# Residual of the one-class tiles: from a VectorE addition to an accumulating scatter into a destination filled beforehand

## What is computed

```
x = x + 0.5 * ffn(layernorm(x), W1, b1, W2, b2)
x = x + attn(layernorm(x), W_toP, W_U, W_F, W_V, W_lam, B_mat, C_mat, W_fromP)
x = x + 0.5 * ffn(layernorm(x), W1, b1, W2, b2)

def ffn(x, W1, b1, W2, b2):              # 8 experts, 128 -> 512 -> 128
    h   = mod(int(x[:, :2].sum(axis=1)), 8)
    sel = [h, mod(h + 1, 8)]             # the class h of a token names its two experts
    return sum over e of  (e in sel) / 2 * (relu(x @ W1[e] + b1[e]) @ W2[e] + b2[e])
```

## Time and profile before

| | us |
|---|---|
| median of three runs | 600.19 |
| lowest and highest run | 599.95, 601.44 |
| span of the profiled execution | 598.6 |
| of it: setup until the first matmul of the first feed-forward stage | 63.0 |
| first feed-forward stage until the last scatter landed | to 269.4 |
| attention stage and second sort | to about 386 |
| second feed-forward stage | to the end |

### The profile page before, as it was taken

The page is one execution under the profiler, slowest core; times in us unless marked ns, Lnnn a source line. Parts: engine busy times, 40 slices in busy tenths (PEclk is TensorE's granted clock), DMA queues, the critical chain, the costliest instruction groups (busy, mean ns, idle before and its releaser), DMA issues.

```text
span 598.6 us, 15962 instructions
## 1 busy us (share of the span) xinstructions
PE 514.1 (86%) x5269; PEld 437.2 (73%) x5269; DVE 432.9 (72%) x1026; ACT 296.2 (49%) x494; POOL 321.1 (54%) x410
## 2 busy tenths in 40 slices
PE   0278899999999999956799836999999999999990
PEld 0136599999999999942466614689999999999980
DVE  6899677777777777746876779677777777777760
ACT  2384655555555556412988400155555655555540
POOL 3014847777777767350016610447777677777543
PEclk9996999999999999997999967699999999999996
DMA  9980111112111112109003380111121111112100
GB/s 244 328 340 11 41 34 50 47 47 50 48 51 43 51 41 53 31 30 266 16 1 72 72 142 1 28 38 46 51 50 48 44 46 47 48 51 51 36 24 18
DMA packets 37850, 40.96 MB, mean 68 GB/s; under 512 B 5813, under 2 KB 30731, under 8 KB 37266
## 3 DMA queue, kind: packets, MB, share of 16 engines
q1 hardware_dynamic: 27698, 21.65, 13.5%
q0 software_dynamic: 9088, 17.87, 11.5%
q10 hardware_dynamic: 992, 0.44, 0.3%
HBM read 23.00 MB, written 17.83 MB: 68 GB/s over the span
## 4 chain that ended last, share of the span: by engine, by line
PE 69%; DVE 14%; issue 5%; DMA 3%; ACT 3%; POOL 3%; SPq 2%; POOLq 0%; DVEq 0%
PE ps L774 19%; PE ps L756 10%; PE ps L758 10%; PE ps L757 10%; PE ps L776 10%; PE ps L792 2%; SPq L366 2%; PE ps L680 2%; PE ps L728 2%; DMA X<-in_L_attn_x 1%; DVE X L1122 1%; DVE bn L1101 1%; POOL G L478 1%; DVE onehot_b L987 1%; PE ps L836 1%
## 5 line engine op out<-in xcount | busy, mean ns | idle before, releaser
L1047 DVE SCALAR_TENSOR_TENSOR hlo<-ps,hhi 128x1024 f16<-128x1024 f32 x144 | 174.1, 1209 | 103.0 <-ACT hhi L586 103.0
L586 ACT ACTIVATE hhi<-ps 128x1024 f16<-128x1024 f32 x144 | 145.7, 1012 | 170.1 <-PE ps L758 170.1
L774 PE MATMUL ps<-w2s,hhi 128*128 x1136 | 202.3, 273 | 0.0
L776 PE MATMUL ps<-w2s,hlo 128*128 x1136 | 194.9, 219 | 0.0
L478 POOL DMA_INDIRECT G<-rows,places x142 | 141.9, 1000 | 88.2 <-issue 40.2
L756 PE MATMUL ps<-xhi,w1s 128*128 128x256 f16 (+1 forms) x736 | 168.0, 248 | 3.9 <-DVE xlo L1041 2.1
L758 PE MATMUL ps<-xhi,w1s 128*128 128x256 f16 (+1 forms) x736 | 168.0, 248 | 0.0
L757 PE MATMUL ps<-xlo,w1s 128*128 128x256 f16 (+1 forms) x736 | 167.9, 248 | 0.0
L774 PEld LDWEIGHTS ps<-w2s,hhi 128*128 128x128 f16 x1136 | 111.1, 98 | 12.1
L776 PEld LDWEIGHTS ps<-w2s,hlo 128*128 128x128 f16 x1136 | 111.1, 98 | 1.3
L486 POOL DMA_INDIRECT x1d<-O,places x71 | 71.3, 1004 | 41.6 <-issue 29.1
(11 more groups left out here) (240 smaller groups left out, 509.5 us busy)
## 6 DMA issues: line engine op xcount, KB each, us to landing
rows<-X SPq DMA_DIRECT2D x2, 2080.0 KB, 12.0
rows<-X SPq DMA_DIRECT2D x4, 1040.0 KB, 7.6
X<-in_L_attn_x SPq DMA_DIRECT2D x8, 512.0 KB, 8.0
X<-x1d SPq DMA_DIRECT2D x8, 512.0 KB, 7.4
G<-rows,places POOLq DMA_INDIRECT x142, 2.6
w1r<-in_L_ffn_W SPq DMA_DIRECT2D x1, 2048.0 KB, 11.3
x1d<-O,places POOLq DMA_INDIRECT x71, 2.3
out<-O,places POOLq DMA_INDIRECT x71, 2.3
```

What stands on the lines that cost most here:

```text
L586: nc.scalar.activation(hhi[tile.k][e][:, :, 0:tile.cols], H[e][:, :, 0:tile.cols], ACT.Relu).then_inc(hi_done[e], 1)
L774: nc.tensor.matmul(Y[tile.k][:, s, :], hhi[tile.k][e][:, c, tok], w, start=first, stop=False, skip_group_check=True)
L776: ins = nc.tensor.matmul(Y[tile.k][:, s, 0:P], hlo[tile.k][e][:, c, tok], wh, start=False, stop=(e == 1 and c == CH - 1), skip_group_check ...
L1047: v.scalar_tensor_tensor(out=hlo[tile.k][e][:, :, c], in0=H[e][:, :, c], scalar=0.0, in1=hhi[tile.k][e][:, :, c], op0=ALU.max, op1=ALU.sub ...
```

## The change

The destination of each scatter is filled with the stage's input before the stage. In the first stage SP copies x from DRAM to `x1d` in one DMA of 4 MB behind the bias parts; in the second SP stores each quarter of X to `out` behind the quarter of `rows`. POOL waits for these copies (`seeded`) after its first eight gathers. For a pure tile the scatter then has an add as its compute operation, so that it adds O to the row in DRAM, and it has no bounds check; DVE's `residual` is left out, and the first step of `collect` takes b2 of the class, spread over both sub-tiles, in place of O. The class's table entry and the wait for the old scatter move with it to `collect`. G of a pure tile is free once `xn` is made. Mixed tiles go on as before.

```diff
+            sp.dma_start(x1d, x.rearrange("b t d -> (b t) d")).then_inc(seeded[0], 16)
             sp.wait_ge(rows_out[0], 32)
+            sp.wait_ge(seeded[0], SEEDED[0])
...
                 sp.dma_start(rows_t[:, s, :], X[:, s, :]).then_inc(rows_out[1], 16)
+                sp.dma_start(out_t[:, s, :], X[:, s, 0:D]).then_inc(seeded[1], 16)
...
                     for s in range(tile.subs):
+                        if tile.pure:
+                            nc.gpsimd.indirect_dma_start(
+                                out=dst, out_offset=bass.IndirectOffsetOnAxis(
+                                    ap=places[:, tile.at, SUB + s:SUB + s + 1], axis=0),
+                                in_=O[tile.slot][:, s, :], in_offset=None,
+                                compute_op=ALU.add).then_inc(scat[tile.slot], 16)
+                            continue
...
                 pool.wait_ge(back_ready, 1 + r)
+                pool.wait_ge(seeded[r], SEEDED[r])
...
-                            pool.wait_ge(res_done, (tile + (AHEAD - SLOTS)).done())
+                            old = tile + (AHEAD - SLOTS)
+                            if old.pure:
+                                pool.wait_ge(xn_ready, old.done())
+                            else:
+                                pool.wait_ge(res_done, old.mixed_done())
...
+                def residual(tile):
+                    if tile.pure:
+                        return
+                    at = ready(tile)
+                    dve.wait_ge(gath[tile.slot], tile.moved())
                     for s in range(tile.subs):
                         ins = v.tensor_tensor(O[tile.slot][:, s, :], G[tile.slot][:, s, 0:D],
-                                              b2v[:, bass.ds(at[0 if tile.pure else s], D)], ALU.add)
+                                              b2v[:, bass.ds(at[s], D)], ALU.add)
                     ins.then_inc(res_done, 1)
...
                     o, y = O[tile.slot][:, 0:tile.subs, :], Y[tile.k][:, 0:tile.subs, :]
+                    base = o
+                    if tile.pure:
+                        base = b2v[:, bass.ds(ready(tile)[0], D)][:, None, :].to_broadcast([P, SUB, D])
                     dve.wait_ge(y_ready, tile.done())
-                    v.scalar_tensor_tensor(out=o, in0=y[:, :, 0:P], scalar=scl[:, 2:3], in1=o, op0=ALU.mult,
+                    v.scalar_tensor_tensor(out=o, in0=y[:, :, 0:P], scalar=scl[:, 2:3], in1=base, op0=ALU.mult,
                                            op1=ALU.add).then_inc(y_half, 1)
```

More of the change, by code:

```diff
@@ L68, in macaron_kernel @@
         rows_t = rows[1:N + 1, :].rearrange("(t p) d -> p t d", p=P)
+        out_t = out.rearrange("b t d -> (b t) d").rearrange("(t p) d -> p t d", p=P)
+        SEEDED = (16, 16 * (NPAIR // 2))
         x1_t = x1d.rearrange("(t p) d -> p t d", p=P)
@@ L237, in macaron_kernel @@
         table_ready = sem("table_ready")
+        seeded = [sem("seeded0"), sem("seeded1")]
         gath = [sem(f"gath{k}") for k in range(SLOTS)]
@@ L293, in done, with mixed_done @@
                 return self.r * NJ + self.j + 1
+            def mixed_done(self):
+                return self.r * MIXED + sum(not Tile(self.r, j).pure for j in range(self.j + 1))
             def moved(self):
@@ L391, in _ @@
                 sp.dma_start(rows_t[:, s, :], X[:, s, :]).then_inc(rows_out[1], 16)
+                sp.dma_start(out_t[:, s, :], X[:, s, 0:D]).then_inc(seeded[1], 16)
             sp.wait_ge(rows_out[1], 16 * NPAIR // 2)
+            sp.wait_ge(seeded[1], SEEDED[1])
             for k in range(SLOTS):
@@ L1049, in low, with ready @@
                                            op1=ALU.subtract).then_inc(lo_done[e], 1)
-                def residual(tile):
-                    at = load(tile.at)
+                def ready(tile):
                     if r == 0 and tile.j == 0:
                         dve.wait_ge(b2_ready, 1)
-                    dve.wait_ge(gath[tile.slot], tile.moved())
                     if tile.j >= SLOTS:
                         dve.wait_ge(scat[tile.slot], (tile + -SLOTS).moved())
+                    return load(tile.at)
+                def residual(tile):
[3 more added lines that the diff above has]
+                    dve.wait_ge(gath[tile.slot], tile.moved())
                     for s in range(tile.subs):
                         ins = v.tensor_tensor(O[tile.slot][:, s, :], G[tile.slot][:, s, 0:D],
-                                              b2v[:, bass.ds(at[0 if tile.pure else s], D)], ALU.add)
+                                              b2v[:, bass.ds(at[s], D)], ALU.add)
                     ins.then_inc(res_done, 1)
```

## The result

| | before | after |
|---|---|---|
| median, us | 600.17 | 620.78 |
| lowest and highest run | 599.95, 601.44 | 619.76, 621.8 |
| ratio, 95% interval | | 1.0342, [1.0324, 1.0359] |
| span of the profiled execution | 598.6 | 619.8 |

The changed kernel is 3.4% slower, some 20 us, far above the forecast of 602.7 and above the range's end of 611.0. The direction was foreseen, the size was not. Of the four runs of the changed kernel two lie near 619.9 and two, the profiled one among them, near 621.7, with a mean granted clock of 0.948 to 0.949 and of 0.943. What follows reads the trace after in the order of the groups of before.

The account below looks back on a forecast made before the run. PE was taken to bound the feed-forward bodies, with POOL close behind. Terms of 0 for the bodies, 0.8 for the tails and 1.7 for the head gave +2.5 us on 600.19, so 602.7, range 599.8 to 611.0.

Parts of the forecast that it names:

- d: Extra POOL issue time of one accumulating scatter over a plain one: taken as +0.1 us, bounded by -0.03 and +1.0.
- POOL as the bound above a threshold: Rival, feed-forward bodies: above d = 0.21 each stage grows by 50 d - 10.4, 621 at d = 0.4; chance 0.15.
- The spare time: POOL in the body: 0.29 us to spare for a tile, 10.4 us over 36 tiles, covering 50 d = 5.
- the lead of the gathers: Body: gathers are issued more than two tiles before ACT needs them, so landings of twice 2.1 us are covered.
- The tail: End of each stage: four of POOL's last seven scatters accumulate, 4 d = 0.4 us for a stage, 0.8 for both.
- The head, +1.7: Start of the first stage: the copy to x1d ends at 61.8, delays tile 0's gathers, costs PE 1.7 us.
- the prediction's other assumption: Copy to x1d: reading and writing cost as much as the slower alone, 9.7 to 14.3 us, ending at 52 to 57.
- The residual: DVE in the bodies: pure tiles lose two additions each, 28.2 us in all, hidden beside PE's work, worth 0.
- The moved waits: G's release by ACT's normalising and the later wait for the old scatter: zero cost.
- the copies to `out`: Before the second feed-forward stage: four stores of 1 MB, covered by 27 us before its first gather, zero cost.
- The last signs that the prediction named: Accumulating scatter's mean against 1007 ns, POOL's idle time ahead of a scatter (0.29 us to spare), ACT waiting for gathers.

## Why the prediction was wrong

**The step that failed is the size of d.** It was bounded by -0.03 and +1.0, and 0.1 was taken, near the low end, because gather and scatter differ by 0.03. That likeness says how little direction and check cost; both rows are plain copies, and neither says anything of an add. The runs showed 0.59, six times the term. With it the prediction's own rival, POOL as the bound above a threshold, became the case, and it had a chance of 0.15. Between bounds that far apart, with a threshold between them and no row of the operation, nearness to a cheap relative was too weak a reason.

**The spare time was a second error, the other way.** The 0.29 us of a tile are right: from the first scatter to the last gather POOL's idle time beyond 0.30 sums to 8.97 us, near the 10.4 taken. What was left out is the lead of the gathers. POOL in the kernel before has three long waits and two shorter ones behind its last gather (237.16), 10.74 us beyond 0.30 in all:

```profile
237.16 0.99 POOL L478 DMA_INDIRECT G<-rows,places  x1 [0.30 <-issue]
...
244.96 0.98 POOL L486 DMA_INDIRECT x1d<-O,places  x1 [3.25 <-PE ps L758]
...
255.80 0.98 POOL L486 DMA_INDIRECT x1d<-O,places  x1 [3.10 <-PE ps L758]
```

This time can be used too, because POOL may fall behind before anyone waits. In the changed kernel its last gather is 16.0 us late, and ACT's last `xn` only 8.8; before and after:

```profile
247.97 0.49 ACT L600 ACTIVATE xn<-G 128x127 f32<-128x127 f32 x1
```

```profile
253.11 1.02 POOL L488 DMA_INDIRECT G<-rows,places  x1 [0.30 <-issue]
```

```profile
256.74 0.49 ACT L622 ACTIVATE xn<-G 128x127 f32<-128x127 f32 x1 [1.68 <-DMA G<-rows,places]
```

The prediction knew this lead ("more than two tiles before ACT needs it") and used it for the transfers alone, not for POOL. So the threshold is at d = 0.39 and not at 0.21. By the rival's formula, 50 d - 10.4, the measured d would have given 19 us for a stage and about 640 in all; its 621 for d = 0.4 is near the result by luck, because the two errors offset each other.

**The tail** was priced as 4 d, 2.3 us at the measured d, and lost 4.1. The rest is a queue: DVE's end finds POOL with five scatters to issue, where it was three with a fourth just begun.

**The head, +1.7, was wrong.** The copy was done before the first gather's data. Stretches of the setup after, columns as in rows 8:

```profile
42.00:44.00 2.00, 0.00 (x0) 0.00 (x0) 1.97 (x4) 2.00 (x2) 0.00 (x0) 1.00 1.77 587
...
54.00:56.00 2.00, 2.00 (x4) 0.96 (x4) 1.75 (x5) 2.00 (x2) 2.00 (x2) 0.50 0.04 8
```

```profile
60.48 0.88 ACT L622 ACTIVATE xn<-G 128x127 f32<-128x127 f32 x2 [1.19 <-DMA G<-rows,places]
```

A stretch counts a packet where it starts, which is how the DMA share comes to 1.77. The trace has the copy as 64 packets of 64 KB: the first starts at 42.3, the last starts at 53.1 and ends at 55.6. So 4.19 MB took 13.3 us, 315 GB/s. Reading and writing did not each cost their own time, and the prediction's other assumption (9.7 to 14.3 us, an end at 52 to 57) was right. SP issued the copy at 37.44, and the profile has its landing 20.0 us later, at 57.4, still ahead of the first gather's data: ACT starts at 60.48, as in rows 10. The transposes of tile 2 start at 70.12 where it was 69.77, but at 69.72 in the kernel without the add, which has the same copy. The Trainium skill, page "DMA: Bandwidth & Descriptors", section "Latency and other measured facts", has 207 GB/s for copies between DRAM tensors in tiles of 128 x 16 KiB at a row pitch of 512 KiB, and 214 at its best pitch. This copy, in runs of 64 KB, went 1.5 times as fast; no run here has the page's layouts.

**What held.** The residual is worth nothing in time, shown by the kernel without the add; DVE's busy time fell by 22 us, not 28: the additions' group fell by 24.1 (34.3 us for 142 of them, 10.2 for 42), since two in a row overlap, and the other 1.8 us are not accounted for. The moved waits and the copies to `out` cost nothing. The last signs that the prediction named were the right ones to look at: the scatter's mean, the idle time ahead of it, and ACT's wait for gathers.

## What to carry to other kernels

An indirect DMA with an add isn't a scatter with a free addition: here it costs POOL 1.6 times the issue of a plain one, and the engine that writes descriptors may be the one that stands closest behind the bound. Before work is moved to such an engine, sum its idle time from the first instruction that will grow to the end of the stage, less the gap that every issue has, and divide by the number of those instructions: that is the price from which it decides. Idle time behind the engine's last gather counted here because the gathers have a lead, about 9 us. If the new instruction's price isn't in the trace and its bounds lie on both sides, measure it or move only as many as the upper bound allows. Here 12 of 25 tiles were free and 25 cost 20 us.

## What the runs showed of the hardware

- The accumulating indirect scatter of 128 rows of 512 B takes 1.59 to 1.60 us on POOL, the plain one 1.01, without bounds check 0.99. With 64 rows the accumulating one takes 1.44. The queue's packets show what is written. These are the rows of POOL's queue (packets, MB, share of 16 engines' span) of the kernel before, the changed one, and the one with 64 rows:

```profile
q0 software_dynamic: 9088, 17.87, 11.5%
```

```profile
q0 software_dynamic: 20288, 17.87, 20.1%
```

```profile
q0 software_dynamic: 13888, 14.59, 15.8%
```

  A plain indirect DMA has 9088 / 284 = 32 packets here. The 100 accumulating ones added 112 each, so they have 144, and with 64 rows 80: one packet for each row and 16 more (in the trace 128 data packets of 512 B where a plain scatter has 16 of 4096 B). The data are the same by the profile's count; in single packets they hold the DMA engines nearly twice as long in all.
- From the last scatter's end to the end of POOL's last instruction, a DRAIN, it is 8.3 us with plain scatters (also in the kernel without the add and in the one with the copies alone), 6.8 to 6.9 with 24 accumulating ones in a stage, 7.1 with 50 of 64 rows, and 5.6 with 50 of 128. It falls with the number of packets on POOL's queue, about 0.24 us for 1000. Why is open; this is the gain of the version with 12 tiles.
- A write of 128x512 numbers by POOL takes 0.56 us and one of 128x688 0.71, and the gap ahead of the next indirect DMA is 0.17 behind it instead of 0.30, so it adds less than its length.
